# An adaptive-norm block with attention and experts on one core: the fill in an order of its own, and the router's logits without a transpose

## The chip, the core and the metric

The kernel runs on one core of a Trainium2 chip. The metric is the time of one execution on the device in microseconds; less is better. PE is TensorE, DVE VectorE, ACT ScalarE, POOL GpSimd, and SP issues nearly all DMAs.

## The reference

Eight batches of 256 tokens with 128 features (`B, S, D`), one block of a transformer, all in fp32:

```python
mod = (silu(c) @ wmod).reshape(8, 6, 1, -1)      # sa, ca, ga, sb, cb, gb; ga, gb kept away from 0
h = layernorm(x) * (1 + ca) + sa
x = x + ga * attention(h, W_qkv, W_o)             # 16 heads of 8, causal, ALiBi
h = layernorm(x) * (1 + cb) + sb
x = x + gb * ffn(h)

def ffn(h):
    probs = softmax(layernorm_gb(h) @ Wr + br)    # 8 experts; gamma, beta inside this norm
    # expert 0 has W1, b1, W2, b2; experts 1..7 all have the same perturbed copy:
    # the largest 5% by |w| are shrunk, the smallest 5% enlarged (w + 0.8 * w * tier)
    y = gelu(h @ W1s + b1s) @ W2s + b2s
    return sum over experts of probs * y
```

Since experts 1 to 7 are equal, only two networks are computed, and their outputs are mixed with probs[0] and the sum of the others. The thresholds of the 5% are order statistics of |W1| and |W2|, 65536 values each, and are found bit by bit.

## The kernel before

The five engines each have a written list of instructions that meet at semaphores. After a short prologue every engine runs `for t in range(T_FIRST, T_END)` with T_FIRST = -10, and constants say at which step each piece stands. One step handles one group of four heads of one batch, so a batch takes four steps (`G`), and the attention runs over steps 0 to 37.

**Per batch**: layer norm statistics on DVE (`ln1`), 1 / deviation and the normed tile on POOL (`rstd`, `normal`; for batch 0 the tile is normed on DVE), two transposes on PE into `psQ` (line 958; "the turn"), scale and shift on ACT into `h1T` (line 617), the projection to q and k (line 965), a split of q and k into three bf16 parts (ACT line 631, DVE line 1343, POOL `lower_parts`; for batch 0 `first_parts` and `first_split`), DMAs of the parts to DRAM and back in stacked form (`write_parts`, `stack`), then the values (PE line 975) and their copy into `Vx` (ACT line 640). All of these share the bank `psQ`, in this order.

**Per step**: three score units (`s_unit`, lines 737 to 747) with maxima on DVE (`maxima`, lines 1161 and 1165); five steps later (E_LAG) the scores again with the maximum subtracted (`e_unit`), exponentials on ACT (line 548), the causal mask on POOL (line 489), and the product with the values (`pv`, lines 790 and 795), whose result is copied, turned and divided.

**The selection** works on bit n in step `SLOT[n]`, from step -2 on: four candidates; one or two counts on DVE (`dve_counts`), two or three on ACT (`sign_count`, line 560; three from bit 2 on); a matmul with ones that adds the partitions (`total`, line 902); the decision on DVE (`decide`, `next_cand`, lines 1142 and 1148). The counts of bit n+1 on DVE stand at the end of step n's decision, those on ACT at the head of the next step.

**Spare matmuls** (`spare`, line 688) multiply ones into an unused bank; in steps before 5 there are two behind each total and four behind the scores.

**The fill** is the prologue and steps -10 to -1: it loads, computes silu(c) and the modulations, handles batch 0 up to its values and batch 1 up to its values, transposes the vectors of parameters (`vectors`, `vector_columns`), forms the router's sums (`router_sums`, `router_constants`) and the gates' rows (`gate_sizes`, `other_mod_rows`, `gate_signs`), and works on bits 0 and 1.

**The router** of pair p (batches 2p, 2p+1; 512 tokens): four transposes bring h2 into `h2T` (`c_pe_h`); `c_pe_l` multiplies wrg (128x8) as weights with h2T as 512 moving columns, logits as rows; ACT copies them to `lgT` (`c_act_l`); `c_pe_t` transposes them back in four pieces, tokens as rows (line 842), and DVE reads those (`router_logits`). Pair 0 does it at steps 33 and 36, the others in the tail, between `f1` (first layer) and `f2` (second layer, line 891). `claim_x` passes the bank `psX` from reader to reader.

Of the kernel before, what the change touches and what calls it, by code (L numbers as in the profile page):

```python
# [39 lines left out]
T_FIRST = -10  # L40
# [3 lines left out]
OWN_SPLIT = 1  # L44
# [8 lines left out]
ROWS_STEP, VEC_STEP, SIZE_STEP, BIAS_STEP, WO_STEP = -3, -4, 7, 31, 7  # L53
# [3 lines left out]
LN1_AT = {-9: 1, -4: 2, 1: 3, 4: 4, 8: 5, 12: 6, 16: 7}  # L57
# [14 lines left out]
L_STEP = 33  # L72
# [15 lines left out]
def adaln_block(nc, x, w_qkv, w_o, w1, b1, w2, b2, gamma, beta, wr, br, c, wmod,  # L88
                k_const, q_const, ident_c, probe_c, parts_dram, rows_dram, out):
    with ExitStack() as ctx:  # L90
# [3 lines left out]
        def sem(name):  # L94
# [115 lines left out]
                 "h2T_psum", "h2T_done", "lgT_done", "lgT_out", "lg_psum", "lg_read", "logit_done", "ex_done",  # L210
# [38 lines left out]
        for name, k in (("sil1", 1), ("sil2", 1), ("silu", 1), ("wq", 1), ("wk", 1), ("sa", 1), ("modT", 1), ("wv", 1),  # L249
                        ("wo", 1), ("cols", 1), ("wrg", 1), ("beta", 1), ("gs", 1), ("all", 1), ("absg", 1), ("maxg", 1),  # L250
                        ("cb", 1), ("cg", 1), ("sgn", 1), ("sgn2", 1), ("rows", 1)):
            count += k
            SETS[name] = count
# [3 lines left out]
        def _(sp):  # L257
# [15 lines left out]
            fixed_rows(0)  # L273
            sp.dma_start(vecs[0:NC, :], b1.rearrange("(c p) -> c p", p=P)).then_inc(q["vec_in"], 16)
# [4 lines left out]
            block_in(2)  # L279
# [100 lines left out]
        def _(gp):  # L380
# [85 lines left out]
            rstd(0, NBLK, 1)  # L466
# [12 lines left out]
            for t in range(T_FIRST, T_END):  # L479
# [15 lines left out]
                if b:  # L495
                    normal(b)
                b = batch_at(t, AT_SPLIT)
                if b is not None and b >= OWN_SPLIT:
                    lower_parts(b)
# [21 lines left out]
        def _(act):  # L521
# [5 lines left out]
            act.activation(c_e[:, :], psQ[:, 0:B], ACT.Exp, scale=-1.0).then_inc(q["act_set"], 1)  # L527

# [34 lines left out]
            def c_act_h(p):  # L563
                act.wait_ge(q["h2T_psum"], p + 1)
                if p >= 2:
                    act.wait_ge(q["f1_done"], 4 * (F1_ORDER.index(2 * p - 3) + 1))
                    act.wait_ge(q["lgT_done"], p - 1)
                act.activation(h2T[:, p % 2], (psE[1] if p >= 2 else psQ)[:, :], ACT.Copy).then_inc(q["h2T_done"], 1)

            def c_act_l(p):  # L570
                act.wait_ge(q["lgT_done"], p + 1)
                if p:
                    act.wait_ge(q["lg_psum"], p)
                act.activation(lgT[:, :], (psE[1] if p else psX)[0:NE, :], ACT.Copy).then_inc(q["lgT_out"], 1)
# [18 lines left out]
            for t in range(T_FIRST, T_END):  # L593
# [17 lines left out]
                if b is not None:  # L611
                    act.wait_ge(q["t_done"], b + 1)
                    if b >= 2:
                        act.wait_ge(q["v_done"], b - 1)
                    if b == 0:
                        act.wait_ge(q["dve_set"], SETS["modT"])
                    act.activation(h1T[:, b % 2], psQ[:, 0:S], ACT.Identity, scale=modT[:, 1, b:b + 1],
                                   bias=modT[:, 0, b:b + 1]).then_inc(q["h1_done"], 1)
                    if b == 0:
                        act.wait_ge(q["w1_in"], 16)  # L620
                        act.activation(w1a[:, :], w1_sb[:, :], ACT.Abs).then_inc(q["act_set"], 1)
                b = batch_at(t - 1, AT_QK)
                if b == 0:
                    first_parts()
                elif b is not None:
                    act.wait_ge(q["qk_done"], b + 1)
                    if b == 2:
                        act.wait_ge(q["q0_written"], 16)
                    if b >= 2:
                        act.wait_ge(part_w[b % 2], 32 * (b // 2))  # L630
                    act.activation(part8[:, b % 2, 0:4:3, :], psQ.rearrange("p (a t) -> p a t", a=2),
                                   ACT.Copy).then_inc(q["hi_done"], 1)
                b = batch_at(t - 1, AT_V)
                if b is not None:
                    act.wait_ge(q["v_done"], b + 1)
                    if b == 0:
                        act.wait_ge(q["pool_set"], POOL_SETS)
                    if b >= 4:
                        act.wait_ge(q["pv_done"], G * (b - 3))
                    act.activation(Vx[:, b % 4, :, :, 0:HD],  # L640
                                   psQ[:, 0:S].rearrange("p (i h d) -> p i h d", i=NBLK, h=NH),
                                   ACT.Copy).then_inc(q["v_out"], 1)
# [6 lines left out]
                if t == L_STEP + 1:  # L649
                    c_act_l(0)  # L650
# [15 lines left out]
            for n in range(1, 2 * NPAIR):  # L666
                gelus(n)
                if n == 1:
                    c_act_l(1)
                elif n in (3, 5):  # L670
                    c_act_h((n + 1) // 2)
                    c_act_l((n + 1) // 2)
# [3 lines left out]
        def _(pe):  # L676
# [27 lines left out]
            spare(2)  # L704

            def vectors():

                pe.wait_ge(q["vec_in"], 16 * 6)
                tr(psS[1][:, 0:NC + 3], vecs[:, :], ident[0:NC + 3, 0:NC + 3]).then_inc(q["pe_set"], 1)
# [8 lines left out]
            def s_unit(t, j):  # L718
# [5 lines left out]
                if m == 0 and j == 0:  # L724
                    pe.wait_ge(q["mask_set"], 2)
                    pe.wait_ge(q["dve_set"], SETS["cols"])
# [91 lines left out]
            def c_pe_h(p):  # L818
# [5 lines left out]
                else:  # L824
                    pe.wait_ge(q["lgT_out"], p)
# [650 lines left out]
```

## Time and profile before

| | |
|---|---|
| Median of 3 runs | 246.72 us (245.69 to 247.44) |
| The profiled execution | 246.49 us |
| Its span, first to last instruction | 244.8 us |
| PE busy | 217.0 us (89%) |
| DVE busy | 195.2 us (80%) |
| ACT busy | 169.4 us (69%) |
| POOL busy | 143.2 us (58%) |
| Mean granted clock of TensorE | 0.993 |

Busy time is the sum of the instructions of an engine; it does not say which engine others waited for. The chain of waits does: it is followed back from the last instruction, each time to what released it. Where the chain stays with one engine, that engine's own order sets the time there.

### The profile page before, as it was taken

The numbers are of one execution on the slowest core, as the hardware profiler recorded it, in microseconds if no ns is written. First come the engines' busy times: TensorE is split into PE (matmuls) and PEld (weight loads), VectorE is DVE, ScalarE is ACT, GpSimd is POOL, SyncE is SP. The second block draws the span as 40 slices with busy tenths as digits, with TensorE's granted clock in tenths as the row PEclk, the third lists the DMA queues.
The fourth block names the chain that finished last, engine by engine and source line by source line (L and its number), as shares of the span: only waits on it lengthen the run. The fifth ranks groups of instructions, "written<-read, shape, count | busy, mean of one in ns | idle before, by whom it ended". The sixth has DMA issues, their size and how long they took to land.

```text
span 244.8 us, 5563 instructions
## 1 busy us (share of the span) xinstructions
PE 217.0 (89%) x1848; PEld 143.6 (59%) x1864; DVE 195.2 (80%) x621; ACT 169.4 (69%) x401; POOL 143.2 (58%) x232
## 2 busy tenths in 40 slices
PE   5898888989988989987979879997998999999993
PEld 2454555655655766564656646664554687764783
DVE  2549999999899999999999888884897394764474
ACT  2336767999999988998968967974668552354220
POOL 7652051495887986997585433563859808190710
PEclk9999999999999979999999999999999999999999
DMA  6544673894843722714431500000000001010011
GB/s 198 102 137 143 162 195 98 210 252 130 201 119 98 173 76 83 187 49 122 119 88 60 139 3 5 0 3 3 3 0 1 3 0 44 3 43 0 3 43 44
DMA packets 19155, 20.45 MB, mean 84 GB/s; under 512 B 1367, under 2 KB 17382, under 8 KB 18062
## 3 DMA queue, kind: packets, MB, share of 16 engines
q1 hardware_dynamic: 18438, 19.76, 30.8%
q10 hardware_dynamic: 688, 0.33, 0.5%
q8 instruction: 15, 0.25, 0.5%
q14 instruction: 14, 0.11, 0.2%
HBM read 14.70 MB, written 5.26 MB: 82 GB/s over the span
## 4 chain that ended last, share of the span: by engine, by line
PE 49%; DVE 30%; ACT 11%; issue 8%; DMA 1%; DVEq 0%; ACTq 0%
PE bank L891 12%; PE bank L873 8%; DVE nmax L1165 8%; PE bank L688 4%; DVE msk L1136 4%; ACT msk L560 4%; PE bank L790 3%; DVE nmax L1161 3%; ACT PT L548 3%; DVE cand L1148 2%; PE bank L965 2%; PE bank L856 2%; PE bank L769 2%; PE bank L836 2%; PE bank L747 2%
## 5 line engine op out<-in xcount | busy, mean ns | idle before, releaser
L489 POOL TENSOR_SCALAR_AFFINE_SELECT PT<-PT 128x256 f32<-128x256 f32 (+1 forms) x96 | 45.3, 486 | 38.1 <-ACT PT L548 36.1
L548 ACT ACTIVATE PT<-bank 128x512 f32<-128x512 f32 x96 | 54.8, 608 | 4.2 <-PE bank L764 2.7
L1165 DVE TENSOR_REDUCE nmax<-bank 128x2 f32<-128x512 f32 x64 | 43.3, 681 | 1.9 <-PE bank L747 1.5
L560 ACT ACTIVATE msk<-w2a,cand 128x512 bf16<-128x512 f32 x60 | 43.0, 729 | 0.0
L462 POOL TENSOR_TENSOR ex<-eul,lg 128x32 f32<-128x32 f32 x4 | 21.7, 5436 | 20.2 <-DVE lg L1227 20.2
L560 ACT ACTIVATE msk<-w1a,cand 128x512 bf16<-128x512 f32 x31 | 22.9, 737 | 6.2 <-DVE cand L1148 5.9
L769 PE MATMUL bank<-Qs,Ks 80*128 80x256 bf16 x128 | 24.8, 276 | 0.7 <-ACT PT L548 0.4
L747 PE MATMUL bank<-Ks,Qs 78*128 78x256 bf16 x128 | 24.5, 274 | 0.0
L1136 DVE TENSOR_SCALAR_CACHE_REDUCE msk<-w1a,cand 128x512 bf16<-128x512 f32 x31 | 23.1, 746 | 1.1
L743 PE MATMUL bank<-mask 128*128 128x256 bf16 x64 | 17.8, 279 | 5.5 <-DVE nmax L1165 4.7
L1161 DVE TENSOR_REDUCE nmax<-bank 128x4 f32<-128x512 f32 x32 | 21.6, 675 | 1.1 <-PE bank L740 0.8
L790 PE MATMUL bank<-PT,Vx 128*32 128x256 f32 x256 | 20.4, 391 | 0.6 <-ACT nmT L609 0.6
L688 PE MATMUL bank<-ones_b 128*128 128x512 bf16 x65 | 18.6, 410 | 0.0
L659 ACT ACTIVATE U<-bank 128x256 f32<-128x256 f32 x32 | 12.6, 394 | 7.0 <-PE bank L795 6.7
L591 ACT ACTIVATE hid<-bank,b1p 128x512 f32<-128x512 f32 x16 | 10.3, 680 | 9.6 <-PE bank L873 9.6
L891 PE MATMUL bank<-w2p,hid 128*128 128x128 f32 x128 | 15.3, 277 | 0.0
L873 PE MATMUL bank<-h2T,w1p 128*128 128x512 f32 x32 | 15.1, 599 | 0.0
L891 PEld LDWEIGHTS bank<-w2p,hid 128*128 128x128 f32 x128 | 14.6, 192 | 0.1
L743 PEld LDWEIGHTS bank<-mask 128*128 128x128 bf16 x64 | 7.2, 112 | 12.7 <-DVE nmax L1165 8.4
L902 PEld LDWEIGHTS bank<-acc,ones_f 128*128 128x128 f32 x62 | 9.2, 188 | 8.8 <-issue 7.0
L807 PE MATMUL bank<-ident,U 128*128 128x128 f32 x64 | 13.5, 294 | 1.0 <-ACT U L659 1.0
L902 PE MATMUL bank<-acc,ones_f 128*128 128x4 f32 x62 | 11.1, 250 | 3.5 <-issue 1.9
(200 smaller groups left out, 511.4 us busy)
## 6 DMA issues: line engine op xcount, KB each, us to landing
Qs<-parts SPq DMA_DIRECT2D x7, 576.0 KB
Ks<-parts SPq DMA_DIRECT2D x7, 576.0 KB
parts<-part SPq DMA_DIRECT2D x7, 384.0 KB, 2.8
rows_bc<-rows_out SPq DMA_DIRECT2D x8, 192.0 KB, 7.9
x_all<-in_x SPq DMA_DIRECT2D x8, 128.0 KB, 7.0
parts<-part SPq DMA_DIRECT2D x8, 128.0 KB, 2.9
out<-ob SPq DMA_DIRECT2D x3, 256.0 KB, 2.3
w_sb<-in_w SPq DMA_DIRECT2D x2, 256.0 KB, 5.1
```

Of the source, the lines that this page charges most:

```text
L489: gp.affine_select(out=v, in_=v, compare_op=ALU.is_ge, fill=0.0, base=0, pattern=[[0, v.shape[1]], [1, P]], channel_multiplier=-1).then_in ...
L548: act.activation(PT[:, e % 2, j], psE[u % 2][:, :], ACT.Exp).then_inc(q["exp_done"], 1)
L560: act.activation(msk[:, col], w[:, :], ACT.Sign, bias=cand[:, col:col + 1].bitcast(F32), scale=-(1.0 - 2.0 ** -24), accum_out=acc[:, col:c ...
L688: mm(psU.rearrange("p (a k) -> p a k", a=HG), ones_b[:, :], ones4, start=True, stop=True)
L747: last = mm(bank[:, i * S:(i + 1) * S], Qs[0:R_S, r, h, P:S], Ks[0:R_S, r, h, :], start=False, stop=True, skip_group_check=True)
L769: last = mm(bank[:, i * S:(i + 1) * S], Ks[0:R_E, r, h, 0:P], Qs[0:R_E, r, h, :], start=True, stop=True, skip_group_check=True)
L790: mm(psO[32 * i:32 * i + 32, 0:S], Vx[:, b % 4, 0, h, :], PT[:, e % 2, 1 + i // 2, (i % 2) * S:(i % 2 + 1) * S], start=True, stop=False, s ...
L873: mm(psF[ch][:, :], wt[:, ch * P:(ch + 1) * P], h2T[:, p % 2], start=True, stop=True).then_inc(q["f1_done"], 1)
L891: last = mm(bank[:, i * P:(i + 1) * P], hid_of(n)[:, ch, i * P:(i + 1) * P], wt[:, ch, :], start=(ch == 0), stop=(ch == NC - 1), skip_grou ...
L1136: last = ve.tensor_scalar(msk[:, col], w[:, :], cand[:, col:col + 1].bitcast(F32), 0.0, op0=ALU.is_lt, op1=ALU.add, accum_out=acc[:, col:c ...
L1161: ve.tensor_reduce(nmax[:, b % 2, 0, HG * g:HG * (g + 1)], bank.rearrange("p (h k) -> p h k", h=HG), axis=AX.X, op=ALU.max, negate=True).t ...
L1165: ve.tensor_reduce(nmax[:, b % 2, 1, h:h + 2], bank.rearrange("p (h k) -> p h k", h=2), axis=AX.X, op=ALU.max, negate=True).then_inc(q["ma ...
```

## The change

**The fill.** T_FIRST goes, the loops begin at step 0, and each engine gets its fill as a written list. `turned`, `projected`, `values`, `scaled`, `high_parts`, `value_copy` and `remainder` are the former bodies of the loop as functions. On DVE the statistics of batch 0 come ahead of the sigmoid of c. On PE three spares follow the turn of batch 0 and four its projection; the rows' product (line 970) follows the values. The counts of bit 0 come right after the split of batch 0; the vectors' columns come after bit 2's counts, the gates' signs ahead of bit 1's decision. The values of batch 1 move into step 0 on PE, the router's sums to step 0, its constants to step 1. SP issues block 0 of x before c, and blocks 1 and 2 earlier. The vectors' transposes go to `psO`.

**The router.** `c_act_l`, `c_pe_t` and `lgT`'s role in them go. `c_pe_l` loads h2T in four pieces of 128 columns as weights and moves wrg's 8 columns; the logits have tokens as rows at once. For pair 0 this stands at step 36 (FFN_STEP - 1), step 33 has nothing.

```diff
             def c_pe_l(p):
                 pe.wait_ge(q["h2T_done"], p + 1)
-                if p == 0:
-                    claim_x((q["lgT_out"], 1))
-                elif p == 1:
-                    pe.wait_ge(q["exp_done"], 3 * G * B)
-                mm((psE[1] if p else psX)[0:NE, :], wrg[:, :], h2T[:, p % 2], start=True, stop=True).then_inc(q["lgT_done"], 1)
-
-            def c_pe_t(p):
-                pe.wait_ge(q["lgT_out"], p + 1)
                 claim_x((q["lg_read"], p + 1))
                 for i in range(4):
-                    last = tr(psX[:, i * NE:(i + 1) * NE], lgT[:, i * P:(i + 1) * P], ident[0:NE, 0:NE])
+                    last = mm(psX[:, i * NE:(i + 1) * NE], h2T[:, p % 2, i * P:(i + 1) * P], wrg[:, :], start=True, stop=True)
                 last.then_inc(q["lg_psum"], 1)
...
# SP
+            block_in(0)
             sp.dma_start(c_in[:, :], c).then_inc(q["c_in"], 16)
-            block_in(0)
             sp.dma_start(wmod_sb[:, :], wmod).then_inc(q["wmod_in"], 16)
+            block_in(1)
             sp.dma_start(w1_sb[:, :], w1).then_inc(q["w1_in"], 16)
             sp.dma_start(w2_sb[:, :, :], w2.rearrange("(c p) d -> p c d", p=P)).then_inc(q["w2_in"], 16)
-            block_in(1)
...
# POOL
+            rstd(NBLK, 2 * NBLK, 2)
+            normal(1)
+            rstd(2 * NBLK, 3 * NBLK, 3)
+            normal(2)
+            lower_parts(1)
+            for t in range(T_END):
...
# ACT
+            scaled(0)
+            first_parts()
+            act.wait_ge(q["w1_in"], 16)
+            act.activation(w1a[:, :], w1_sb[:, :], ACT.Abs).then_inc(q["act_set"], 1)
+            value_copy(0)
+            sign_count(0, 2, w1a)
+            scaled(1)
+            sign_count(0, 3, w2a)
+            high_parts(1)
+            sign_count(1, 2, w1a)
+            sign_count(1, 3, w2a)
+            for t in range(T_END):
...
                 b = batch_at(t - 1, AT_V)
                 if b is not None:
+                    value_copy(b)
...
# PE
+            turned(0)
+            spare(3)
+            projected(0)
+            spare(4)
+            values(0)
+            mm(psE[1][0:B, 0:512], c_s[:, :], wmod_sb[:, 2 * D:6 * D], start=True, stop=True).then_inc(q["pe_set"], 1)
+            turned(1)
+            spare(2)
+            projected(1)
+            spare(2)
+            total(0)
+            spare(4)
+            vectors()
+            total(1)
+            spare(2)
+            for t in range(T_END):
...
+                if t == 0:
+                    values(1)
                 b = batch_at(t, AT_T)
                 if b is not None:
+                    turned(b)
...
# DVE
+            first_split()
+            v.wait_ge(q["w2_in"], 16)
+            then_self(absolute(w2a[:, :], w2_sb.rearrange("p c d -> p (c d)")))
+            first_cand()
+            dve_counts(0)
+            gate_sizes()
+            ln1(2)
+            decide(0)
+            next_cand(0)
+            dve_counts(1)
+            after_next(0)
+            remainder(1)
+            other_mod_rows()
+            gate_signs()
+            decide(1)
+            next_cand(1)
+            dve_counts(2)
+            after_next(1)
+            vector_columns()
+            for t in range(T_END):
```

## Rows read from the trace of the kernel before

**Rows 1.** The page, part 4: shares of the chain that ended last, by engine.

```profile
PE 49%; DVE 30%; ACT 11%; issue 8%; DMA 1%; DVEq 0%; ACTq 0%
```

**Rows 2.** The chain of waits in the fill: start us, us, what.

```profile
7.33 0.85 PE bank L688 x2
8.18 0.46 PE bank L958 x2
...
9.28 2.07 PE bank L965 x4
11.36 1.81 PE bank L970 x2
13.16 2.11 PE bank L688 x8
15.27 0.45 PE bank L975 x4
...
17.92 0.86 PE bank L965 x4
```

**Rows 3.** Windows: from:to, us, busy per engine (instructions), PEclk, DMA share, GB/s.

```profile
0.00:23.80 23.80, 19.09 (x74) 9.92 (x75) 13.21 (x54) 9.13 (x21) 12.96 (x39) 1.00 0.54 149
```

**Rows 4.** Timeline of the fill: start us, us, engine, line, operation, [idle before].

```profile
0.79 0.40 SPq L266 DMA_DIRECT2D c_in<-in_c  x1
...
1.25 0.42 SPq L264 DMA_DIRECT2D x_all<-in_x  x1
...
6.12 0.72 POOL L403 TENSOR_TENSOR rs<-ve,mhalf 128x2 f32<-128x2 f32 x1
...
10.36 0.39 DVE L1043 TENSOR_SCALAR w2a<-w_sb 128x512 uint32<-128x512 uint32 x1
...
12.72 0.44 DVE L1090 TENSOR_TENSOR part<-resid,part 128x256 bf16<-128x256 f32 x1
```

**Rows 5.** Timeline of ACT and DVE, 17 to 27 us: bits 0 to 3.

```profile
17.66 0.72 ACT L560 ACTIVATE msk<-w1a,cand 128x512 bf16<-128x512 f32 x1 [0.26 <-DVE cand L1130]
...
20.34 0.72 ACT L560 ACTIVATE msk<-w1a,cand 128x512 bf16<-128x512 f32 x1 [0.68 <-DVE cand L1148]
...
23.16 0.72 ACT L560 ACTIVATE msk<-w1a,cand 128x512 bf16<-128x512 f32 x1 [1.30 <-DVE cand L1148]
...
24.31 0.41 DVE L1108 TENSOR_SCALAR n<-bank 8x256 f32<-8x256 f32 x1
...
25.06 0.41 DVE L1112 TENSOR_TENSOR lgT<-lgT,n 8x256 f32<-8x256 f32 x1
...
25.29 0.36 ACT L640 ACTIVATE Vx<-bank 128x256 f32<-128x256 f32 x1
...
26.37 0.72 ACT L560 ACTIVATE msk<-w1a,cand 128x512 bf16<-128x512 f32 x1 [0.72 <-DVE cand L1148]
```

**Rows 6.** The chain of waits, steps 0 and 1.

```profile
24.13 0.39 PE bank L740 x4
...
25.49 0.36 PE bank L902 x2
...
27.82 0.22 PE bank L958 x2
...
28.70 0.36 PE bank L902 x2
```

**Rows 7.** Timeline of POOL at step 34.

```profile
173.35 2.38 POOL L453 TENSOR_SCALAR n<-x_all,mv,rs 128x128 f32<-128x128 f32 x2
```

**Rows 8.** The chain of waits, first pair of the tail.

```profile
188.92 3.84 PE bank L891 x32
192.76 0.95 PE bank L836 x2
...
197.35 0.34 PE bank L842 x4
```

**Rows 9.** Timeline of PE in the fill: fp32 with 8 columns moving.

```profile
18.76 0.37 PE L716 MATMUL bank<-wr_sb,woTg 128*128 128x8 f32 x2
```

More of the change, by code:

```diff
@@ L494, in _ @@
                 b = batch_at(t, AT_N1)
-                if b:
+                if b is not None:
                     normal(b)
                 b = batch_at(t, AT_SPLIT)
-                if b is not None and b >= OWN_SPLIT:
+                if b is not None:
                     lower_parts(b)
@@ L902, in total, with turned, projected, values @@
                 mm(psX[:, 0:4], ones_f[:, :], acc[:, :], start=True, stop=True).then_inc(q["tot_done"], 1)
-            for t in range(T_FIRST, T_END):
+            def turned(b):
+                pe.wait_ge(q["n1_done"], b + 1)
+                if b == 0:
+                    pe.wait_ge(q["dve_set"], SETS["silu"])
+                else:
+                    pe.wait_ge(q["v_out"], b)
+                for i in range(NBLK):
+                    last = tr(psQ[:, i * P:(i + 1) * P], n1[:, b % 2, i, :], ident[:, :])
+                last.then_inc(q["t_done"], 1)
+            def projected(b):
+                pe.wait_ge(q["h1_done"], b + 1)
+                for a in range(2):
+                    bank = psS[1][:, 0:S] if a and b == 0 else psQ[:, a * S:(a + 1) * S]
+                    last = mm(bank, wqkT[:, a, :], h1T[:, b % 2], start=True, stop=True)
+                    if a == 0 and b == 0:
+                        last.then_inc(q["q0_done"], 1)
+                last.then_inc(q["qk_done"], 1)
+            def values(b):
+                pe.wait_ge(q["res_done"], b + 1)
+                for i in range(NBLK):
+                    last = mm(psQ[:, i * P:(i + 1) * P], h1T[:, b % 2, i * P:(i + 1) * P], wvT[:, :], start=True, stop=True)
+                last.then_inc(q["v_done"], 1)
+            turned(0)
[14 more added lines that the diff above has]
+            for t in range(T_END):
                 n = sel_bit(t)
@@ L1060, in _ @@
             ds(ve.tensor_tensor(c_s[:, :], psQ[:, 0:B], c_e[:, :], op=ALU.mult))
-            ln1(0)
+            v.wait_ge(q["neg_mean"], 1)
+            v.wait_ge(q["ln_rstd"], 1)
+            for i in range(NBLK):
+                last = ve.tensor_scalar(n1[:, 0, i, :], x_all[:, 0, i, :], nm1[:, i:i + 1], rs1[:, i:i + 1],
+                                        op0=ALU.add, op1=ALU.mult)
+            last.then_inc(q["n1_done"], 1)
             v.wait_ge(q["pe_set"], 2)
@@ L1079, in _ @@
             ds(ve.tensor_copy(woT[:, :], psO[:, 0:P]))
+            ln1(1)
             def first_split():
@@ L1312, in perturb_b2, with remainder @@
                 tiers(psX[:, 0:P], psX[:, P:2 * P], b2_bc[:, :], b2p_bc[:, :], b2t[:, :], K_B2, "b2p_done")
-            for t in range(T_FIRST, T_END):
+            def remainder(b):
+                v.wait_ge(q["hi_done"], b + 1)
+                v.wait_ge(q["split_done"], b)
+                pq = psQ.rearrange("p (a t) -> p a t", a=2)
+                ve.tensor_tensor(resid[:, :, :], pq, part8[:, b % 2, 0:4:3, :], op=ALU.subtract).then_inc(q["res_done"], 1)
+            first_split()
[18 more added lines that the diff above has]
+            for t in range(T_END):
                 n = sel_bit(t)
```

170 lines of the change are left out of this document (53 added, 117 removed).

## The prediction

> **What bounds the kernel now.** I read the page first: the chain that ended last is half TensorE, a third VectorE, an eighth ScalarE and almost no DMA [rows 1]. No single engine can be relieved; what counts is what stands on the chain in the stretches that the change touches. There are three: the fill (0 to 23.8 us), steps 33 to 36 (166 to 189 us), and the FFN tail (189 to 242 us). So next I read the chain of waits in each.
>
> In the fill the chain is TensorE from 3 us to 19 us, and the reader should see the pace: two spare matmuls of 512 columns take 0.85 us at 7.3 us, eight of them 2.11 us at 13.2 us, and the same projection (four passes of 256 columns) takes 2.07 us at 9.3 us but 0.86 us at 17.9 us [rows 2]. 512 columns in 0.43 us is the level of 1.2 GHz; 256 columns in 0.215 us is 2.4 GHz. The clock column of the windows says 1.00 for all of it [rows 3], so here the pace is the witness: the array ran at the lower level until about 13.7 us, after the dense work that began at 9.3 us.
>
> Then come the bits of the selection. One bit is: candidate, counts on DVE and ACT, total on PE, decision on DVE. In the timeline of ACT and DVE the counts of bit 1, 2 and 3 start at 20.34, 23.16 and 26.37 us [rows 5]. From the total of bit 2 (25.49) PE walks to the total of bit 3 (28.70) nearly without a gap [rows 6]. From there on step follows step, and whatever is late at bit 3 is late at the end.
>
> In the tail PE works from 188.9 to 240.9 us without a hole: each pair of batches after the first pays 0.95 us for the logits' product and 0.34 us for their four transposes back, between the large products [rows 8].
>
> **Part 1, the tail.** Per pair the product (0.95, and 0.01 behind it) and the transposes (0.34) go [rows 8], 1.30 us. In their place stand four fp32 matmuls with 8 columns moving and 128x128 of h2T as weights. An fp32 matmul is two passes, so eight loads of weights. Price from both sides. Below: L891 does 32 passes with fresh 128x128 fp32 weights in 3.84 us [rows 8], 0.12 or a little less each, and that with 128 columns moving; eight give 0.9 us. Above: the two passes of L716, the same shape as the new ones, take 0.37 us from the first start to the last end [rows 9], latency of the end included; eight at 0.185 give 1.5 us. I take 0.9, since L891 runs in a stream, as the new ones will. Saving 0.4 us per pair, three pairs, 1.2 us; ends 0.4 x 3 = 1.2 gained and 0.2 x 3 = 0.6 lost. ScalarE's copy of the logits goes too, at nothing: it has only gelus to do there and PE is behind it. The logits also come earlier to DVE, and POOL's power behind them starts earlier with them, so nothing is uncovered there.
>
> By rule and row: L891's rows show one load per 0.12 us, so a load is hidden behind the pass before it. The Trainium skill, "TensorE: Matmul & The Clock Gate", in Part 3, says that a load of weights overlaps matmuls in flight only when its row group differs; here all use the full array, so by it the eight would not be hidden and this part would lose. In this trace the full-array stream of L891 speaks against it.
>
> **Part 2, pair 0 inside the loop.** Step 33 loses the product (0.95 us), step 36 trades 0.34 us for 0.9. PE gains 0.95 for a while, but the attention's weights need POOL's mask first, and POOL is in the norm of batch 6 from 173.35 for 2.38 us [rows 7], which doesn't move. About 0.5 us comes through and 0.55 is given back: between 0.4 gained and 0.3 lost. I take 0.2 gained.
>
> **Part 3, the fill.** Step by step.
> (a) c is issued behind block 0 of x: one issue of 0.46 us (0.79 to 1.25) [rows 4]. The five spares queue behind c's transpose, so PE is 0.46 later: the weights' transposes and the modulation end at 7.8 instead of 7.33 us.
> (b) The statistics move ahead of c's sigmoid on DVE. POOL's 1 / deviation was ready at 6.84 as it stands [rows 4], so the normed batch 0 is there by 7.8, when PE comes to it. Its turn: 0.46, to 8.2. From the turn's end to the projection, through ScalarE's scaling, it was 0.64 (8.64 to 9.28 [rows 2]): 8.85. But three spares stand there, 3 x 0.43 = 1.3, to 9.5. The projection, 2.07, ends at 11.6 against 11.36 [rows 2]. The gap that was the wait is filled with spares: nothing gained, 0.25 lost.
> (c) The split ends at 13.4 instead of 13.16 [rows 4]. Now the gain: |W2| (0.39) and the first candidate come at once, not after the vectors' columns, so the first counts start near 13.95, against 17.66.
> (d) PE from 11.6: four spares (0.86 fast, 1.72 slow; I take 1.5, the rise somewhere in them), values (0.45), the rows' product (half of 1.81 at the fast level, 0.9), the turn of batch 1 (0.22): to 14.7. ScalarE's first sign ends by then (0.72 and its readout), its scaling takes the 0.64 again: projection from 15.35 (0.86), two spares (0.43), total of bit 0 at 16.7; the second sign on ScalarE is done by 16.3. From a total's start to the next counts it is 0.88 us (25.49 to 26.37 [rows 5, 6]). So bit 1 counts at 17.6, not 20.34.
> (e) From bit 1's counts to bit 2's it was 2.82 us (20.34 to 23.16): two counts, the remainder of batch 1, two rows, the decision. Now the gates' signs stand in there as well, which stood behind bit 2's counts: 24.31 to 25.47, 1.16 us [rows 5]. Bit 2 counts at 17.6 + 2.82 + 1.16 = 21.6: 1.55 us ahead of 23.16. The vectors' columns and the first maxima follow on DVE in the 2.13 us in which ScalarE makes its three signs (23.16 to 25.29), and bit 2's total starts at 21.6 + 2.33 (23.16 to 25.49 [rows 6]) = 23.95.
> (f) The price. The values of batch 1 move from before step 0 to its end on PE, but their copy stays at the end of ScalarE's step 0, ahead of bit 3's signs. Before, the copy ran in idle time at 25.29 [rows 5]. Now: total 23.95, then 2.33 us of scores and spares (25.49 to 27.82 [rows 6]), 0.45 of values, 0.4 of copy: ScalarE reaches bit 3 at 27.15, against 26.37. So the total of bit 3 is 0.8 us **later** than before, PE idle ahead of it. Turning batch 2 waits for the same copy, and the router's sums (now after it) fit into that idle time.
> SP's order moves block 1 and block 2 of x ahead of weights; w1 and w2 are needed only from 12.9 on, so this costs nothing; without this cover it would be one block's transfer, under 1 us. The stacking of batch 0 moves back by 0.25 us while step 0 moves forward; its first scores were at 24.13 without a wait for it [rows 6]. Now they have until 23.4 before bit 2's total feels them; if the data really landed only at 23.8, it would cost 0.6. I take nothing, since PE was busy with other work until 24.08 and nothing says that the data came so late.
> Fill: 0.8 lost.
>
> **Sum.** 0.8 - 0.2 - 1.2 = -0.6 us. The profiled execution took 246.49 us itself (span 244.8), so it gives 245.9; the median is 0.2 above that execution. I forecast **246.0**.
>
> **Rivals.**
> A, the array is fast sooner. The pauseless run now begins at 3.3 us and has no wait at 8.6. If the spares behind the first turn already take 0.22 us, the projection starts at 8.85 and takes 0.9 to 1.0: it ends 1.7 us earlier and all bits with it. Against it: PE was at work before 8.64 too, and the turn at 8.18 was still slow, 0.46 for two passes that take 0.22 later [rows 2, 6]. -0.6 - 1.7 = -2.3: 244.2. Chance 0.18.
> B, the array is fast later, and the change is slower. If the level of 1.2 GHz lasts through the turn of batch 1, spares (1.72), values (0.9), rows (1.81) and turn (0.46) take 4.9 us from 11.6, not 3.15: every bit 1.75 us later on top of the wait in (f). -0.6 + 1.75 = +1.15: 247.6. It decides from the point where the four spares after the first projection take 1.7 us together. Chance 0.13.
> C, the exchange of operands does not do what it says: the loads aren't hidden and eight cost 1.5 us. Tail +0.6, pair 0 +0.3, fill +0.8: +1.7, 248.2. Speaking for it, L716's 0.37; against it, L891. Chance 0.09. The rule on row groups that stands under part 1 in the Trainium skill, "TensorE: Matmul & The Clock Gate", Part 3, would lead here.
> D, the wait in (f) does not form, because the copy is reached before bit 3's candidate is there. Then the 1.55 us of (e) stay: -1.55 - 0.2 - 1.2 = -2.95, 243.5. For it speaks only that before it formed nowhere; the order of the diff speaks against it. Chance 0.1.
> My forecast 0.5.
>
> **The numbers.** From no change a measurement tells about 1%, 2.5 us: below 244.2 or above 249.2. Faster by more: D, half of A, which lies on the bound, and little else: 0.2. Slower by more takes B and C together (+3.4), or a conflict that I don't see in steps 0 to 4, where three engines alternate: 0.1. Same 0.7. The range reaches from D to C: 243.5 to 248.3.
>
> **What would show it.** (1) L836's and L842's counterpart: four matmuls, 0.9 us in the tail per pair. (2) The copy into Vx of batch 1 at step 0, with ScalarE idle before it for some 3 us, waiting for PE; PE idle for 0.4 us before the turn of batch 2 and near 1 us before the total of bit 3. (3) Counts of bit 0 near 14, of bit 2 near 21.6. (4) The first projection at 2.07 us. I am wrong if ScalarE doesn't wait in (2), if bit 3's counts start before 26.4, or if (1) takes over 1.2 us.

## The result and the profile after

The changed kernel took 249.56 us (median of 14 executions, 246.68 to 250.17) against 246.88 us of the kernel before beside it (14 executions). The ratio is 1.0094, 95% interval 1.0059 to 1.013: slower, above the range of the forecast. The profiled execution took 249.59 us (span 247.8), 3.10 us more than that of before. The experiments below have their own runs of the kernel before beside them (medians 246.4 to 247.0 us), and their ratios are to those. A ratio leaves out executions more than 1.5% above the fastest of the same kernel, which the medians keep; in e6_signs_values that is four of ten (245.67 to 246.04 us).

The page of the changed kernel, parts 1 and 2, and then the clock's row of the kernel before:

```profile
PE 213.5 (86%) x1859; PEld 144.9 (58%) x1859; DVE 196.3 (79%) x622; ACT 168.4 (68%) x397; POOL 142.6 (58%) x231
...
PEclk9997679999999999999999999999999999999999
```
```profile
PEclk9999999999999979999999999999999999999999
```

PE has 3.5 us less work, and the span is 3 us longer. What is new is the 7, 6, 7 in the fourth to sixth slice of the clock (18.6 to 37 us). The kernel before has one dip too, the 7 in its fifteenth slice (86 to 92 us). Windows of the changed kernel (columns as in [rows 3]) place it:

```profile
0.00:20.00 20.00, 14.21 (x54) 7.98 (x55) 11.44 (x46) 8.43 (x19) 10.99 (x37) 1.00 0.57 147
20.00:24.80 4.80, 0.69 (x7) 0.31 (x4) 4.25 (x14) 2.23 (x6) 1.86 (x2) 0.69 0.85 227
24.80:26.00 1.20, 1.14 (x4) 0.70 (x5) 0.47 (x3) 0.00 (x0) 0.00 (x0) 0.50 0.49 146
26.00:28.00 2.00, 2.00 (x9) 1.21 (x8) 1.71 (x5) 0.00 (x0) 0.00 (x0) 0.50 0.67 103
...
32.00:33.00 1.00, 0.87 (x4) 0.62 (x5) 0.24 (x3) 0.49 (x2) 0.00 (x0) 0.55 0.81 197
33.00:35.00 2.00, 2.00 (x9) 1.14 (x8) 1.68 (x6) 1.88 (x5) 0.00 (x0) 0.50 0.71 172
```

From 20 to 24.8 us PE is busy for 0.69 us of 4.8. When it resumes, the granted clock is 0.50, the level of 1.2 GHz, until after 28 us, and it falls a second time at 32 us. The timeline of PE there, changed kernel:

```profile
10.36 1.66 PE L923 MATMUL bank<-h1T,wqkT 128*128 128x256 f32 x4
...
19.44 0.35 PE L905 MATMUL bank<-acc,ones_f 128*128 128x4 f32 x2 [1.02 <-DVE msk L1163]
...
24.86 0.56 PE L905 MATMUL bank<-acc,ones_f 128*128 128x4 f32 x2 [4.17 <-ACT msk L594]
...
27.36 1.69 PE L699 MATMUL bank<-ones_b 128*128 128x512 bf16 x4
28.89 0.61 PE L932 MATMUL bank<-wvT,h1T 128*128 128x128 f32 x4
...
32.13 0.56 PE L905 MATMUL bank<-acc,ones_f 128*128 128x4 f32 x2 [0.86 <-issue]
```

L905 is `total` (L902 in the kernel before). The reader should see the 4.17 us without work before bit 2's total, and four spares that then take 1.69 us where they take about 1.03 at full pace. ScalarE in the same stretch, with the wait that step (f) priced:

```profile
22.53 0.72 ACT L594 ACTIVATE msk<-w1a,cand 128x512 bf16<-128x512 f32 x1 [3.19 <-DVE cand L1175]
...
29.53 0.39 ACT L559 ACTIVATE Vx<-bank 128x256 f32<-128x256 f32 x1 [4.77 <-PE bank L932]
29.81 0.72 ACT L594 ACTIVATE msk<-w1a,cand 128x512 bf16<-128x512 f32 x1
```

VectorE and POOL ahead of bit 1's decision (the gates' signs are L1135, L1137 and L1139; the decision is L1169):

```profile
17.42 0.16 DVE L1169 TENSOR_TENSOR cond<-bank,ktab 128x4 uint32<-128x4 f32 x1 [0.30 <-PE bank L905]
...
20.97 1.25 DVE L1139 TENSOR_TENSOR lgT<-lgT,n 8x256 f32<-8x256 f32 x1
22.16 0.14 DVE L1169 TENSOR_TENSOR cond<-bank,ktab 128x4 uint32<-128x4 f32 x1
```
```profile
20.67 1.28 POOL L422 TENSOR_TENSOR part<-resid,part 128x512 bf16<-128x512 f32 x1
```

The product of the signs takes 1.25 us here; before it took 0.41 [rows 5]. And the tail's chain, first pair, against [rows 8]:

```profile
194.37 3.84 PE bank L894 x32
198.21 0.79 PE bank L845 x8
199.00 3.54 PE bank L876 x8
202.53 3.57 PE bank L894 x32
```

L845 is the router's product, eight passes in 0.79 us.

I read the offset to the kernel before at marks that both have: the moment of each bit's decision on DVE (`cond`). It is -2.55 us at bit 0 (17.42 against 19.97), -0.59 at bit 1, -0.55 at bit 2, **+3.53** at bit 3, **+5.14** at bit 4, and then stays, to +5.12 at the last bit. Steps 33 to 36 add 0.3; the tail gives back 2.4 (from the last residual of the attention to the last output 50.67 us, before 53.05). That leaves 3.05 at the last output.

### The profile page after: what moved, and what is told of

Read it like the earlier page. It is cut to its first block, busy times and chain, and to the rows that moved or that the text cites. A ratio compares the mean times of both kernels' runs of the same rounds, so it can differ in the third digit from the quotient of the medians.

```text
span 247.8 us, 5559 instructions
## 1 busy us (share of the span) xinstructions
PE 213.5 (86%) x1859; PEld 144.9 (58%) x1859; DVE 196.3 (79%) x622; ACT 168.4 (68%) x397; POOL 142.6 (58%) x231
## 4 chain that ended last, share of the span: by engine, by line
PE 42%; DVE 34%; ACT 11%; issue 8%; POOL 2%; DVEq 0%; ACTq 0%; POOLq 0%
PE bank L894 12%; PE bank L876 7%; DVE nmax L1192 7%; ACT msk L594 5%; DVE msk L1163 4%; DVE nmax L1188 3%; PE bank L800 3%; PE bank L699 2%; DVE cand L1175 2%; PE bank L923 2%; PE bank L757 2%; ACT PT L582 2%; DVE resid L1346 2%; DVE h L1223 2%; PE bank L753 2%
## 5 line engine op out<-in xcount | busy, mean ns | idle before, releaser
L492 POOL TENSOR_SCALAR_AFFINE_SELECT PT<-PT 128x256 f32<-128x256 f32 (+1 forms) x96 | 46.0, 495 | 36.6 <-ACT PT L582 34.6
L1188 DVE TENSOR_REDUCE nmax<-bank 128x4 f32<-128x512 f32 x32 | 21.6, 677 | 4.9 <-PE bank L750 4.8
L757 PE MATMUL bank<-Ks,Qs 78*128 78x256 bf16 x128 | 25.4, 281 | 0.0
L753 PE MATMUL bank<-mask 128*128 128x256 bf16 x64 | 18.4, 287 | 7.2 <-DVE nmax L1192 5.5
L905 PE MATMUL bank<-acc,ones_f 128*128 128x4 f32 x62 | 11.6, 257 | 7.1 <-ACT msk L594 4.2
L699 PE MATMUL bank<-ones_b 128*128 128x512 bf16 x52 | 17.6, 459 | 0.0
L905 PEld LDWEIGHTS bank<-acc,ones_f 128*128 128x128 f32 x62 | 9.7, 196 | 12.3 <-issue 11.0
L894 PEld LDWEIGHTS bank<-w2p,hid 128*128 128x128 f32 x128 | 14.8, 192 | 1.4 <-issue 1.4
L894 PE MATMUL bank<-w2p,hid 128*128 128x128 f32 x128 | 14.9, 275 | 0.0
```

What stands on the lines that cost most here:

```text
L492: gp.affine_select(out=v, in_=v, compare_op=ALU.is_ge, fill=0.0, base=0, pattern=[[0, v.shape[1]], [1, P]], channel_multiplier=-1).then_in ...
L753: mm(bank.rearrange("p (h k) -> p h k", h=2)[:, :, P:S], mask5[:, HG, :], mask5[:, 0:2, :], start=True, stop=False, skip_group_check=True)
L757: last = mm(bank[:, i * S:(i + 1) * S], Qs[0:R_S, r, h, P:S], Ks[0:R_S, r, h, :], start=False, stop=True, skip_group_check=True)
L894: last = mm(bank[:, i * P:(i + 1) * P], hid_of(n)[:, ch, i * P:(i + 1) * P], wt[:, ch, :], start=(ch == 0), stop=(ch == NC - 1), skip_grou ...
L1188: ve.tensor_reduce(nmax[:, b % 2, 0, HG * g:HG * (g + 1)], bank.rearrange("p (h k) -> p h k", h=HG), axis=AX.X, op=ALU.max, negate=True).t ...
```

## The experiments

One table serves all. The columns from "bit 0" on are of the profiled execution: when bit 0 is decided, and then the time from each decision to the next. They leave out when the fill began.

| kernel | ratio to before (95%) | bit 0 | 0 to 1 | 1 to 2 | 2 to 3 | 3 to 4 |
|---|---|---|---|---|---|---|
| before | 1 | 19.97 | 2.78 | 3.25 | 3.20 | 3.78 |
| after | 1.0094 (1.0059 to 1.013) | 17.42 | 4.74 | 3.29 | 7.28 | 5.39 |
| e1_router_alone | 0.9891 (0.9818 to 0.9963) | 19.24 | 2.79 | 3.25 | 3.19 | 3.79 |
| e2_busy | 0.9942 (0.9901 to 0.9982) | 15.43 | 4.74 | 3.09 | 5.41 | 3.95 |
| e3_values_early | 0.997 (0.9929 to 1.0011) | 17.25 | 4.74 | 3.29 | 5.88 | 3.73 |
| e4_signs_back | 0.9996 (0.9958 to 1.0034) | 15.28 | 2.80 | 3.71 | 6.48 | 3.96 |
| e5_busy_values | 0.9843 (0.979 to 0.9897) | 15.56 | 4.75 | 3.09 | 3.61 | 3.72 |
| e6_signs_values | 0.9861 (0.982 to 0.9902) | 17.49 | 2.80 | 3.71 | 4.69 | 3.72 |
| e7_signs_values_busy | 0.9802 (0.9752 to 0.9851) | 15.05 | 2.81 | 3.71 | 3.20 | 3.85 |
| e8_busy_values_dma | 0.9882 (0.9841 to 0.9923) | 15.77 | 4.74 | 3.09 | 3.61 | 3.72 |
| e9_before_idle | 0.9999 (0.9968 to 1.0029) | 17.43 | 2.81 | 3.34 | 4.86 | 3.58 |
| e10_before_signs | 1.0187 (1.0138 to 1.0236) | 19.25 | 4.73 | 3.25 | 4.73 | 3.58 |
| e11_before_signs_busy | 1.0072 (1.0036 to 1.0108) | 20.67 | 4.72 | 3.09 | 3.25 | 3.76 |
| e12_busy_remainder | 0.9947 (0.991 to 0.9985) | 17.07 | 3.91 | 3.52 | 5.40 | 3.96 |

**e1_router_alone**: the kernel before with the router's part of the change only (the diff of `c_pe_l` shown ahead, with its copies and semaphores).

> The kernel before with the change of the router's logits alone; the fill as before. Theory (the tail gained, the fill lost): from 188.9 us to the end the changed kernel was 2.4 us shorter than the kernel before and in steps 33 to 36 it was 0.3 us longer, so this kernel takes 2.1 us less than the kernel before, about 244.8 us, ratio 0.991. Rival (the tail gains only since it starts late, with DVE and POOL ahead of it): 0.5 to 1 us less. Rival (my forecast's price): 1.4 us less.

Measured: 243.84 us (4 executions), ratio 0.9891. From the last residual to the last output it takes 50.66 us, as the changed kernel does (50.67). So the tail's gain is all the router's, 2.4 us, and it stands alone; the fill is what costs, some 5 us (1.0094 against 0.9891). The 0.3 us of steps 33 to 36 is the router's as well: from the last bit's decision to the last residual it is 29.64 us here, 29.66 in the changed kernel and 29.35 before.

**e2_busy**: the changed kernel, with PE kept at work before bit 2's total.

```diff
+                if t == 0:
+                    spare(18)
                 if n is not None and t < E_LAG:
                     total(n)
```

> The changed kernel with 18 spare matmuls more on PE, between the first scores of step 0 and the total of bit 2, where PE stood idle for 4.2 us and the granted clock went to 0.50 behind it. Theory (the idle time costs by the clock): no clock under 1.00 from 20 to 36 us, the total of bit 2 where it was (24.9), bit 3's signs near 28.1 instead of 29.8, the total of bit 3 near 30.4 instead of 32.1, bit 4's near 33.9 instead of 37.2; all behind it 3.3 us earlier, about 246.3 us. Rival (the clock is only a symptom, the copy of batch 1's values is the cost): the total of bit 3 stays above 31.5 and the time above 248.5.

Measured: 244.13 us, clock 1.0 throughout. Timeline of PE in e2_busy, against 24.86 and 32.13 of the changed kernel:

```profile
18.52 4.05 PE L699 MATMUL bank<-ones_b 128*128 128x512 bf16 x18
22.87 0.36 PE L905 MATMUL bank<-acc,ones_f 128*128 128x4 f32 x2 [0.30 <-issue]
...
25.04 0.61 PE L932 MATMUL bank<-wvT,h1T 128*128 128x128 f32 x4
...
28.27 0.35 PE L905 MATMUL bank<-acc,ones_f 128*128 128x4 f32 x2 [0.85 <-issue]
```

With more work on PE and no wait taken away, bits 2 to 3 take 5.41 instead of 7.28 us and bits 3 to 4 take 3.95 instead of 5.39: 3.3 us by the clock alone, second fall included. The ratios say 3.7, and the profiled executions differ by 5.8, since this one also began its fill 2.0 us earlier (bit 0 at 15.43 against 17.42). The 5.41 that is left against 3.20 is the wait of step (f).

**e3_values_early**: the values of batch 1 back ahead of step 0, where PE has nothing to do.

```diff
             total(1)
             spare(2)
+            values(1)
...
-                if t == 0:
-                    values(1)
```

> The changed kernel with the values of batch 1 on PE ahead of step 0 again (behind the total of bit 1 and its spares), so that their copy on ACT no longer waits for the end of step 0. Theory (both: the clock fell and the copy waits): the clock still falls at 22 to 25 us; ACT goes from its copy into bit 3's signs at 25.9, PE reaches the total of bit 3 at about 30.3 instead of 32.1 behind its slow scores and spares: 1.8 us less, and up to 3 us less if the second fall of the clock at 32 us does not come: 246.6 to 247.8. Rival (the copy's wait does not decide): under 0.5 us less.

Measured: 245.68 us. The clock still falls (L905 at 24.69 after 3.74 us without work), but only once, and bits 2 to 3 take 5.88. What is left over 3.61 (e5_busy_values) is the half pace, 2.3 us. So the two costs are separate: this edit takes away the copy's wait, and the second fall with it (bits 3 to 4 in 3.73), and leaves the first.

**e4_signs_back**: the gates' signs back behind bit 2's counts.

```diff
-            gate_signs()
             decide(1)
             next_cand(1)
             dve_counts(2)
             after_next(1)
+            gate_signs()
```

> The changed kernel with the gates' signs on DVE behind bit 2's counts again, as before. Theory: the decision of bit 1 comes at 20.3 instead of 22.2, the total of bit 2 at 23.0; PE is idle 2.3 us instead of 4.2, too short for the clock to fall: 1.9 us by the order and 3.3 by the clock, about 244.5 us. Rival (the clock falls all the same): 1.9 us less, 247.7. Rival (bit 2 has slack): no change, 249.6.

Measured: 246.56 us. Bits 0 to 1 take 2.80 again, bits 1 to 2 take 3.71 instead of 3.29: 1.94 - 0.42 = 1.5 us gained there. But PE still has a hole of 2.28 us, and the clock still falls, so the theory that this is too short for it is refuted:

```profile
20.82 0.51 PE L905 MATMUL bank<-acc,ones_f 128*128 128x4 f32 x2 [2.28 <-issue]
21.19 1.01 PE L699 MATMUL bank<-ones_b 128*128 128x512 bf16 x2
...
27.88 0.36 PE L905 MATMUL bank<-acc,ones_f 128*128 128x4 f32 x2 [0.85 <-issue]
28.10 0.59 PE L699 MATMUL bank<-ones_b 128*128 128x512 bf16 x2
```

Bits 2 to 3 take 6.48 us against 5.41 in e2, which has the same wait for the copy: 1.1 us is the price of this fall. The last two rows matter too. They stand behind the same waits as the second fall of the changed kernel (0.56 us before the turn of batch 2, 0.85 before the total of bit 3), and behind a first fall as well, and yet the spares run at full pace.

**e5_busy_values**: e3's edit and 16 spares where e2 has 18.

> The changed kernel with both cures: the values of batch 1 ahead of step 0, and 16 spares in PE's wait before the total of bit 2. Theory (two independent costs, the clock about 4 us and the copy's wait 2.2 us once the clock is held): from the decision of bit 2 to that of bit 3 3.2 us, as in the kernel before, instead of 5.4 with the busy array alone; 2.2 us less than that kernel: about 242 us. Rival (one cost, told twice): as the kernel with the busy array alone, 244 us.

Measured: 242.93 us (4 executions). Clock 1.0, bits 2 to 3 in 3.61. Against e2's 5.41 the copy's wait is 1.8 us, and 0.2 more in the next bit. From the start of bit 2's total to that of bit 3's it is 3.19 us (23.01 to 26.20), as before (3.21). The 0.4 that stays above 3.20 between the decisions lies on VectorE: it decides bit 3 behind the row maxima, 0.81 us after the total starts, and bit 2 0.39 us after.

**e6_signs_values**: e3's and e4's edits together, no spares added.

> The changed kernel with the gates' signs behind bit 2's counts and the values of batch 1 ahead of step 0, no spares added. PE then has some 1.8 us without work before the total of bit 2. Theory: that is short enough for the clock if the fall needs about as long as in the changed kernel (4.2 us) or e4 (2.3 us, where it fell): bit 2's decision near 21.7 if the array starts fast, bit 3's 3.2 us later, 241.5 us. Rival (the clock falls at this length too, as the gaps of 1 us before the total of bit 1 add up): bit 3's decision 5 us after bit 2's, 243.5 us.

Measured: 243.73 us. It gains against e3 and e4, but the clock is not saved, as the rival had it: the hole of PE has shrunk to 1.84 us, and after it the two spares take 1.01 us instead of 0.59.

```profile
23.03 0.38 PE L905 MATMUL bank<-acc,ones_f 128*128 128x4 f32 x2 [1.84 <-issue]
23.27 1.01 PE L699 MATMUL bank<-ones_b 128*128 128x512 bf16 x2
```

**e7_signs_values_busy**: e6 with eight spares ahead of bit 2's total.

> The kernel of e6 with 8 spares (1.7 us) in PE's wait before the total of bit 2. Theory: clock 1.00 throughout, bits 2 and 3 as early as the order allows: 241 us, the best of all. Rival: the early fill is given back at step 4 or 5 (batch 1's stacked parts, row maxima), and it is no better than e5.

Measured: 241.63 us (4 executions, 239.94 to 242.69), ratio 0.9802: faster than both kernels. Bits 2 to 3 take 3.20 us, as before. e6's 4.69 against 3.20 is the price of the half pace once more, 1.5 us. The early fill is not given back later, as the rival had it: from bit 4 to the last output it is 206.85 us, in e5 206.87. This is the version to keep, though its lead over e5 rests on four executions each, whose intervals overlap (0.9752 to 0.9851 and 0.979 to 0.9897), and on the decisions 0 to 4, which take 13.57 against 15.17 us.

**e8_busy_values_dma**: e5 with SP's DMAs in the old order (c ahead of block 0, block 1 behind w2).

> The kernel of e5 with SP's first transfers in the order of the kernel before (c, block 0, wmod, w1, w2, block 1). Theory: the first matmul starts at 2.8 us instead of 3.6 and the modulations at 6.0 instead of 6.9 to 7.5, all behind them 0.5 to 1 us earlier: e5 less 0.5 to 1. Rival (the projection of batch 0 depends on when the array reaches its full clock, and on nothing that the transfers move): no difference.

Measured: 243.97 us; the intervals are e5's to 0.01 us, and bit 0 is decided at 15.77 against 15.56. PE begins at 2.81 instead of 3.68 us, but then waits for wmod and later for batch 1's norm:

```profile
6.50 0.58 PE L711 MATMUL bank<-c_s,ob 128*128 128x8 f32 x4 [0.55 <-DMA ob<-in_wmod]
...
12.96 0.44 PE L915 MATMUL bank<-ident,n 128*128 128x128 f32 x2 [0.34 <-POOL n L410]
```

So SP's new order costs nothing at the end, as the forecast had it. The profiled execution is 1.07 us slower than e5's; 0.2 of it is the start, and 0.9 comes behind bit 4 (207.78 against 206.87 us to the last output), where its granted clock falls once more (0.60 from 128 to 132 us) and e5's doesn't.

**e9_before_idle**: the kernel before, without spares ahead of step 0.

```diff
                     total(n)
-                    spare(2)
+                    if t >= 0:
+                        spare(2)
...
-                if AT_QK < t < E_LAG:
+                if 0 <= t < E_LAG:
```

> The kernel before with the six spare matmuls left out behind each of the first two totals (bits 0 and 1); the spares from step 0 on stay. It touches no data and no wait. My theory: the granted clock falls when PE has long had no work. Here PE would stand still for 2 us or so from 19.5 to 22 us and again before 25.5. If the clock falls from this (0.50 in some stretch between 20 and 30 us), the turn, scores, totals and counts of steps 0 to 2 come at half pace and the whole is 2 to 4 us slower than before, near 249.5. Rival: the clock stays, then no change, 246.4, since spares hold up nothing; the loss in the changed kernel would then have to be in its waits alone.

The edit takes away more than its expectation says: the 16 spares of steps -6 to -3 go too. Measured: 246.47 us against 246.85, no change, and yet the clock did fall. Windows of e9, then PE:

```profile
15.00:16.00 1.00, 1.00 (x6) 0.90 (x6) 1.00 (x6) 0.82 (x3) 0.38 (x1) 1.00 0.23 84
16.00:16.80 0.80, 0.45 (x5) 0.35 (x3) 0.80 (x5) 0.80 (x3) 0.00 (x0) 0.81 0.35 126
16.80:17.40 0.60, 0.56 (x2) 0.50 (x2) 0.55 (x2) 0.38 (x1) 0.00 (x0) 0.50 0.48 143
...
18.00:20.00 2.00, 0.55 (x3) 0.52 (x3) 2.00 (x7) 1.35 (x4) 0.01 (x1) 0.50 0.75 224
...
24.00:26.00 2.00, 2.00 (x9) 1.15 (x8) 1.71 (x5) 2.00 (x5) 0.00 (x0) 0.50 0.78 189
```
```profile
16.84 0.56 PE L902 MATMUL bank<-acc,ones_f 128*128 128x4 f32 x2 [0.40 <-ACT msk L560]
19.45 0.56 PE L902 MATMUL bank<-acc,ones_f 128*128 128x4 f32 x2 [2.05 <-ACT msk L560]
```

Bits 2 to 3 take 4.86 instead of 3.20, 1.66 us lost to it. But bit 0 is decided 2.5 us earlier than in the kernel before. Of this 0.9 is the start, which differs from execution to execution (the first projection is done at 10.43 against 11.29 us), and 1.7 comes from the spares that had stood ahead of the values and of the second turn, in the way. The two nearly cancel. The run shows that idle time on PE brings the fall in this kernel too, and that spares on the chain have a price. It doesn't show that one long hole is needed: the clock is at 0.50 at 16.84 us already, behind waits of 0.56, 0.50 and 0.40 us, and the 2.05 us come after it. One thing stays open: two of the twelve executions show a mean granted clock of 1.00, and they are the slowest (248.84 and 248.99 us); they were not profiled.

**e10_before_signs**: the kernel before with the signs moved ahead of bit 1's decision, that part of the change alone. **e11_before_signs_busy**: the same with eight spares ahead of bit 2's total.

```diff
+                if t == ROWS_STEP + 2:
+                    gate_signs()
                 if n is not None:
                     decide(n)
                     next_cand(n)
...
-                if t == ROWS_STEP + 2:
-                    gate_signs()
```

> The kernel before with one thing of the change alone: the gates' signs stand ahead of bit 1's decision on DVE instead of behind bit 2's counts. Bit 1's decision can wait for them: they are 1.16 us of work, and DVE has 0.2 to 0.3 us free there, so bit 2 is decided some 0.9 to 1.1 us later than before. Two theories on what that costs at the end: the move alone, as priced, 1 us (247.4). Move and clock, as in the changed kernel: PE has no work for some 2 us before bit 2's total; if the clock falls from that, 1 and 1.5 to 3 us, 249 to 250.

> The kernel before with the gates' signs ahead of bit 1's decision, and with eight more spare matmuls (1.7 us) ahead of bit 2's total, so that PE isn't idle there. The clock should stay: 1 us slower than before for the move on DVE (247.4), and 1.5 to 3 us faster than the same without the spares, if those lose the clock. If both give the same time, PE's idle time cost nothing here.

Measured: 250.87 us (6 executions), ratio 1.0187, and 248.54 us, ratio 1.0072. PE in e10, then in e11:

```profile
26.67 0.51 PE L902 MATMUL bank<-acc,ones_f 128*128 128x4 f32 x2 [2.87 <-ACT msk L560]
...
29.13 1.53 PE L688 MATMUL bank<-ones_b 128*128 128x512 bf16 x4
```
```profile
25.05 1.89 PE L688 MATMUL bank<-ones_b 128*128 128x512 bf16 x8
28.09 0.35 PE L902 MATMUL bank<-acc,ones_f 128*128 128x4 f32 x2 [1.14 <-issue]
...
29.40 1.03 PE L688 MATMUL bank<-ones_b 128*128 128x512 bf16 x4
```

One moved helper on DVE makes the kernel before 1.9% slower, more than the whole change did. Eight useless matmuls take more than half of that back by the ratios (1.15%, 2.8 us), and bits 2 to 3 go from 4.73 to 3.25, 1.5 us. The two sizes don't agree: the profiled execution of e10 is its fastest (248.80 us, its median is 250.87) and decides bit 0 1.4 us before e11's, which takes the same 248.78 us. So e10 against e11 shows the clock's fall and its sign; for the size I take the 1.5 us. What is left in e11 is the move on DVE: 1.94 us in bits 0 to 1, not 1.16.

**e12_busy_remainder**: the changed kernel with 14 spares, and with the remainder of batch 1 behind the signs, so that POOL's work on it comes later.

```diff
-            remainder(1)
             other_mod_rows()
             gate_signs()
+            remainder(1)
             decide(1)
```

> The changed kernel with spares ahead of bit 2's total (14, so that PE isn't idle and they are done before the total comes), and with the remainder of batch 1 on DVE moved from ahead of the gates' rows and signs to behind them. Wherever the signs stood ahead of bit 1's decision, their last product took 1.25 us on DVE and not 0.41, and ran beside POOL's TENSOR_TENSOR of 1.28 us on the parts of batch 1, which the remainder sets off. My theory: the two hold each other up, and that is why bit 1 took 4.74 us from decision to decision and not the 3.98 that I had priced. Then here the product takes 0.41 us, decision to decision is 3.9 us, and the whole is 0.85 us faster than with spares alone (0.9942 of before; so 0.991, 243.3 to 244 if the before is at 246.5). Rival: the product is that slow by itself in this place (its operands, or what stands ahead of it): then 4.74 us again and no gain.

Measured: 245.59 us, ratio 0.9947, the same as e2's 0.9942. The mechanism is confirmed, the gain at the end isn't. DVE, then POOL, in e12:

```profile
20.04 0.41 DVE L1141 TENSOR_TENSOR lgT<-lgT,n 8x256 f32<-8x256 f32 x1
...
20.98 0.14 DVE L1171 TENSOR_TENSOR cond<-bank,ktab 128x4 uint32<-128x4 f32 x1
21.15 0.59 DVE L1177 SCALAR_TENSOR_TENSOR cand<-cond,nxt 128x4 uint32<-128x4 uint32 x1
```
```profile
21.12 0.61 POOL L420 CAST part<-resid 128x512 bf16<-128x512 f32 x1 [1.98 <-DVE resid L1348]
```

The product takes 0.41 us away from POOL's instruction, and bits 0 to 1 take 3.91, the forecast's 3.98. But now the candidate, four columns wide, meets POOL's cast and takes 0.59 us instead of 0.16, so bits 1 to 2 take 3.52 instead of 3.09. Decisions 0 to 2 take 7.43 us against e2's 7.83: net 0.4 us, too little for this measurement.

## Why the prediction was wrong

The step that failed is the price of PE's idle time in (e) and (f) of part 3. The waits were seen, and PE's standing still in them was put at nothing; its clock fell to 0.50 behind them, which cost 3.3 us by e2. A smaller miss is the size of the signs' move in (e), 0.74 us too little. The fill, +0.8 us in the sum, measured +5.1.

- **(a) to (d), the fill up to bit 1**: right in the sum, in part by luck. The projection starts 0.9 later than forecast (10.36; c was there at 3.68, and PE waited for it), but takes 1.66 and not 2.07 us, since the array rises to full pace within it; it ends at 12.0 (forecast 11.6). Bit 1's counts start at 17.81 (forecast 17.6). The same order starts them at 15.82 in e2, so the hit belongs to the profiled execution. On the pace, the prediction's pair of 0.43 us for 512 columns and 0.215 us for 256 mixes types: the first are bf16 spares, the second an fp32 projection. Spares take 0.22 us each at full pace (18 in 4.05 us in e2), so 512 columns in bf16 go from 0.43 to 0.22 us.
- **(e), the signs ahead of bit 1's decision**: mis-sized. Bit 2's counts start at 22.53, not 21.6. The 1.16 us came from rows in which nothing of POOL's ran beside the product [rows 5]; at the new place it ran beside POOL's 1.28 us and took 1.25 instead of 0.41 us. From bit 1's counts to bit 2's it was 4.72 us, forecast 3.98: +0.74, and 0.2 came from (a) to (d). e12 shows the cause. The kernel before shows the same effect just ahead of its signs, where the prediction didn't read it; `nxt` takes 0.16 us at 21.68 and 27.05:

```profile
23.84 0.55 DVE L1152 TENSOR_TENSOR nxt<-cand,probe 128x4 uint32<-128x4 uint32 x1
```
```profile
23.20 1.16 POOL L425 TENSOR_TENSOR part<-resid,part 128x512 bf16<-128x512 f32 x1
```

- **(e) and (f), PE's idle time**: priced at nothing, and this is the main error. From 20.7 to 24.86 us PE had no work, since the values of batch 1 had moved out of that stretch and the signs had made it longer. The clock fell to 0.50, cost 1.7 us by bit 3's signs (from bit 2's total to them 4.95 us, forecast 3.2), and the next bit took 1.6 more than before (5.39 against 3.78), 1.4 of it by a second fall (3.95 in e2). e2 takes both back with spares alone; e9 and e10 bring the fall about in the kernel before.
- **(f), the copy behind the wait**: right in place and size. Priced at 2.35 us from bit 2 to bit 3; e2 against before shows 2.2, and 0.2 in the next bit. Rival D fell with it: the wait forms.
- **The sum of the fill**: 0.8 (forecast) + 0.2 (a to d) + 0.75 (e) + 1.75 + 1.6 (clock) = 5.1, measured 5.14 at bit 4.
- **Part 1, the tail**: right in sign, and forecast at half its size: 2.4 us instead of 1.2. The eight passes take 0.79 us (0.9 forecast), which gives 0.5 per pair. The other 0.3 lies in neighbours that I had left at their old prices: the first layer's product is 3.54 instead of 3.63 us, and the second layer's product behind it is 3.57 instead of the 3.77 that it took behind the four transposes (before and after, same line and count).
- **Rival C and the row groups**: refuted. The router's eight passes with 8 columns moving take 0.79 us (L845), 0.10 each; the 32 with 128 columns moving take 3.57 us (L894), 0.11 each. Every pass has a fresh load of the full array. At the projection's pace (256 columns in 0.215 us [rows 2]) 128 columns are 0.107 us of moving, an estimate, and yet they add only 0.01 us to a pass. So load and matmul run beside each other in L894's stream; of the router's eight alone one couldn't tell, since 8 columns are next to nothing. The rule that the Trainium skill, "TensorE: Matmul & The Clock Gate", has in Part 3, that only loads to another row group overlap, does not describe this stream; e1 shows the gain by itself.
- **Part 2, pair 0**: forecast -0.2, measured +0.3, the wrong way and at the edge of its bounds. e1 has the same 0.3 without the new fill. The eight passes stand on the chain at step 36 and take 0.95 us there, where the four transposes took 0.34 (0.61 more, forecast 0.55), so of the 0.95 us saved at step 33 about 0.3 came through instead of 0.5. Why so little was not tested.
- **Rivals A and B**: A's fill exists. In e7 the first projection starts at 8.41 us and takes 1.13. The changed kernel's own executions fall into two groups, six at 246.68 to 248.1 us and eight at 249.5 to 250.2; the profiled one is of the second. That the first group has A's fill fits the 2 us, but it was not profiled. B had the right subject, the clock, in the wrong stretch: it looked at the rise at the start, not at a fall behind it.

The whole: -0.6 + 4.3 (e and clock) - 1.2 (tail) + 0.5 (pair 0) = +3.0, measured +3.1 between the profiled executions.

## What to carry to other kernels

When a piece of work moves out of a wait of PE, or a piece of DVE's work moves ahead of something that PE waits for, write down how long PE then has nothing at all to do. A hole of 1.8 to 4.2 us cost another 1.1 to 3.3 us here, in work at half pace behind it, on the path that sets the end, and in e9 the fall came behind three waits of about 0.5 us. Spares belong in such a hole and should end before the real work is ready; on the chain they cost (some 1.7 us in the kernel before, by e9). And price a moved instruction by its new neighbours: the same DVE product is 0.41 or 1.25 us, by what POOL does beside it.

## What was not expected of the hardware

- **The clock falls after short holes.** PE's clock fell to 0.50 at the work that followed 4.17 (after), 3.74 (e3), 2.87 (e10), 2.28 (e4) and 1.84 us (e6) without a matmul; it stayed at 1.00 across the wait of 1.14 us in e11 and of 0.30 us in e2. Long holes are not needed: in e9 it fell by 16.8 us, behind waits of 0.56, 0.50 and 0.40 us, and in the kernel before it was at 0.50 from 89 to nearly 92 us, with a wait of 1.01 us before 87.1 and none from there. The second fall of the changed kernel, at 32 us, came after waits of 0.56 and 0.86 us, and e2 and e12 have waits of 0.56 and 0.85 there without a fall. An earlier fall alone doesn't make the difference, since e4 has one, and the same two waits behind it, and keeps 1.00. What does is open, and I read no rule from these lengths.
- **DVE and POOL exclude each other on small work.** A DVE instruction with two operands in SBUF waits out POOL's: 8x256 in 1.25 instead of 0.41 us beside POOL's 1.28, 128x4 in 0.59 instead of 0.16 beside POOL's cast of 0.61 (after, e12), and 128x4 in 0.55 instead of 0.16 beside POOL's 1.16 (before). The Trainium skill, "SBUF — State Buffer", section "Who interferes with whom", says that such an instruction contends with one of GpSimd that reads SBUF and that the later one blocks; these rows agree, down to four columns.
- **The fill's start is not the same twice.** e10 and e11 have the same instructions up to bit 2, and bit 0 is decided at 19.25 and 20.67 us. In e10 the first projection takes 1.51 us from 9.04 on, in e11 2.07 us from 10.05 on, with a granted clock of 0.98 and 1.00 up to 10 us: the array reaches full pace at another moment. Over all profiled fills of the new order bit 0 is decided between 15.05 and 17.49 us. For this reason the table compares intervals, and differences of 1 us between two ratios with few executions are not read.
